# One-hots of a pair of edge chunks 8 to 56 nodes wide by its place in the list, and 88 counted rows for 90

## The chip, the cores and the metric

The kernel runs on one core of a Trainium2 chip. The metric is the device time of one execution in microseconds. PE is the matrix engine (its weight loads are listed apart, as PEld), DVE the vector engine, ACT the scalar engine, POOL the GpSimd engine and SP the engine that here only issues DMAs.

## What is computed

A graph layer on 12,500 nodes with 64 features and 400,000 edges, sorted by their target node `dst`. Targets are drawn as 12500·u², so low nodes have many edges and high nodes few.

```python
msg = node_feat[src] + edge_feat
agg = segment_sum(msg, dst, num_segments=12500)
h = relu(agg @ W1 + b1)
y = h @ W2 + b2
out = layernorm(x + y)
```

## The kernel before

The edge list is cut into 625 **chunks** of 640 edges, five chunks to a **row**, 125 rows. Since the list is sorted, the targets of one chunk lie in a short run of nodes from the chunk's first one.

Edge features are always summed by chunk. For a chunk, DVE writes a **one-hot** (edge by node of the run, `mark`, L887), PE multiplies the chunk's edge features with it (`products`, L1134) into PSUM, and DVE adds the result onto the run's columns of the transposed sums `lists` (`add`, L912). The one-hot's width is `w`: the run of nodes it can hold. Two chunks make a pair, with one `mark` and one interleaved series of products; two pairs make a **quad**, after whose marks DVE may fetch the first nodes of a new row into registers (`load_offsets`, L901, a register load whenever a chunk number is a multiple of 5). The adds of a quad are issued ahead of the marks of the next quad.

The node features `x[src]` of a chunk come in one of two ways. The last chunks of the list (175 before) are **gathered**: POOL issues five indirect DMAs for each (L613), and PE multiplies two operands, `gmsg` and `xmsg`, with the one-hot. The first `CROWS` rows are **counted**: no row of `x` is fetched. Instead, DVE compares each target's slice of the list with node numbers (`make_slot`, two compares L943 and L947 a slot, up to 12 passes of one node or 6 of two), PE turns these into counts of sources per target (`count_piece`, L1152), ACT copies the counts out of PSUM (L737), and PE multiplies them, in blocks of up to 128 targets, with `x` split in three bf16 parts (`multiply`, L1169, 98 matmuls a block). There are 647 slots in 43 groups of up to 128 passes, and 52 blocks.

One order is planned for all engines (`timeline`). It walks the slots; at some slots (`JOBS_AT`) a quad stands ahead of the slot, and the gathers (`GATHERS_AT`) are spread over the slots by a planned pace `PACE` per gathered chunk. Every engine runs its own part of that order, tied by semaphores: `RING` = 3 slots deep for one-hots of slots, 5 gathered and 6 counted chunks deep for edge data. For each group POOL also issues one indirect DMA for the `records` (L622), three slots behind the DVE search (L839, L844) that gives its offsets.

In the kernel before, a pair is `SLIM` = 32 wide if it is counted and in the first 76 rows, otherwise 64. All gathered pairs are 64 wide. A pair that proves wider than its one-hot is found at the start (`over`, L870) and sends the whole sum through a slow loop at the end. After the last slot come the last block's 98 matmuls, the signs that decide on this loop, and then the two dense layers and the norm (L1237 on), which the change does not touch.

Lines of the trace: 887 one-hots, 901 register loads, 912 adds, 943 and 947 compares of a slot, 1134 products by chunk, 1152 counting, 1169 blocks, 613 gathers, 622 records.

Of the kernel before, what the change touches and what calls it, by code (L numbers as in the profile page):

```python
# [8 lines left out]
P = 128  # L9
LN_EPS = 1e-5  # L10
PARTS = 3
TOP = 256
CROWS = 90
SLOT = 12
FINE = 16
RARE = 1e-7
PACE = 7.4

Unit = namedtuple("Unit", "first width nodes block row passes")
Slot = namedtuple("Slot", "group col n width key_cols pieces")  # L20
# [81 lines left out]
def narrow_chunks(n_nodes, n_edges, chunk, wide, most):  # L102

    before = lambda n: n_edges * math.sqrt(min(n, n_nodes) / n_nodes)
    count = 0
    while count < most:
        at = chunk * (count + 1)
        node = math.ceil(n_nodes * ((at + 5.5 * math.sqrt(at * (1 - at / n_edges))) / n_edges) ** 2)
        mean = before(node + wide) - before(node + 1)
        tail = mean - chunk  # L110
        if tail <= 0 or math.exp(-tail * tail / (2 * mean)) > RARE:
            break
        count += 1
    return count
# [42 lines left out]
def build(nc, x, src, dst, edge_attr, w1, b1, w2, b2, out):  # L157
    f32, i32, i16, bf16 = mybir.dt.float32, mybir.dt.int32, mybir.dt.int16, mybir.dt.bfloat16
    f16 = mybir.dt.float16
    ALU, ACT, AX = mybir.AluOpType, mybir.ActivationFunctionType, mybir.AxisListType  # L160

    N, D = x.shape
    E = src.shape[0]
    HID = w1.shape[1]
    TILES = 5
    CHUNK = P * TILES
    NCH = E // CHUNK
    ROWS = NCH // TILES
    ROW = TILES * CHUNK
    RT = TILES * TILES  # L170
    CCH = CROWS * TILES
    GCH = NCH - CCH
# [3 lines left out]
    SHIFT = 6  # L176
    WIN = 1 << SHIFT
    NWIN = -(-N // WIN)
    SLIM = WIN // 2
    NARROW_ROWS = narrow_chunks(N, E, CHUNK, SLIM, CCH) // TILES  # L180
    width_of = lambda kind, i: SLIM if kind == "count" and (i | 1) < NARROW_ROWS * TILES else WIN

    HI = -(-N // P)
    LOG_P = P.bit_length() - 1
# [8 lines left out]
    FINES = ROW // FINE  # L193
    CFINE = CROWS * FINES
    UNITS, SLOTS, WINDOWS, RANGES = plan(N, E, COUNTED, HI)
# [8 lines left out]
    DENSE = [u for u, x in enumerate(UNITS) if max(x.passes) * P > TOP]  # L204
# [70 lines left out]
    with ExitStack() as ctx:  # L275
        def sb(name, shape, dt=f32):
            return ctx.enter_context(nc.sbuf_tensor(name, shape, dt))
# [13 lines left out]
        counts = [sb(f"counts{k}", [P, HI * P], bf16) for k in range(2)]  # L291
        x_parts = sb("x_parts", [P, HI * XC], bf16)
        degrees = sb("degrees", [P, BLOCKS])
        over = sb("over", [P, len(DENSE) + TILES])
        rel_t = sb("rel_t", [P, NCH * TILES], i16)
        idx_t = sb("idx_t", [P, GCH * TILES], i32)
        idx_redo = sb("idx_redo", [P, TILES], i32)
# [21 lines left out]
        span_i = sb("span_i", [ROWS, TILES], i32)  # L319
# [18 lines left out]
        stage = x_parts[0:ROWS, 0:HI * PARTS * D].bitcast(f32)  # L338
        src_f, hi = stage[:, 0:ROW], stage[0:CROWS, ROW:2 * ROW]
        record_out = counts[0][0:CROWS, 0:FINES * REC].bitcast(f32).rearrange("t (b k) -> t b k", k=REC // 2)  # L340
        pad_out = onehot[0][:, 0:5 * REC // 2]
# [38 lines left out]
        src_copied, src_scaled, wide_seen = sem("src_copied"), sem("src_scaled"), sem("wide_seen")  # L380
# [86 lines left out]
        def _(sp):  # L467
# [22 lines left out]
            sp.wait_ge(most_made, 1)  # L490
            for a, b in in_sixteens(CROWS):
                sp.dma_start(most_dram[a * FINES:b * FINES].rearrange("(t k) -> t k", k=FINES), most[a:b, :]).then_inc(most_out, 16)
# [9 lines left out]
            sp.wait_ge(records_made, 2)  # L502
            for a, b in in_sixteens(CROWS):
                sp.dma_start(record_dram[a * FINES:b * FINES, :].rearrange("(t b) k -> t (b k)", b=FINES),
# [297 lines left out]
        def _(dve):  # L802
# [54 lines left out]
            for g in range(EARLY_GROUPS):  # L857
# [9 lines left out]
            nc.vector.tensor_scalar(chunk_out[:, 0, :], span_i[:, :], SHIFT, None, ALU.arith_shift_right).then_inc(chunk_made, 1)  # L867
            nc.vector.tensor_copy(chunk_out[:, 1, :], least[:, :]).then_inc(chunk_made, 1)
            dve.wait_ge(over_zeroed, 1)
            nc.vector.tensor_scalar(over[0:NARROW_ROWS, len(DENSE):], span_i[0:NARROW_ROWS, :], float(SLIM), None,  # L870
                                    ALU.is_ge).then_inc(wide_seen, 1)
            subtract(0)
            dve.wait_ge(turned["rel"], NTURNS["rel"])
            nc.vector.memset(lists[:, 2 * ROW:3 * ROW], 0.0).then_inc(agg_zeroed, 1)
# [83 lines left out]
            for s in range(NS + 1):  # L958
# [20 lines left out]
                if s in (3, 7):  # L979
                    k = s // 4  # L980
# [4 lines left out]

            dve.wait_ge(unit_kept, len(EVICTED))
            dve.wait_ge(unit_checked, len(DENSE))
            dve.wait_ge(wide_seen, 1)
            dve.wait_ge(degrees_kept, BLOCKS)
            dve.wait_ge(signs_made, 2)  # L990
            nc.vector.tensor_reduce(signs[:, 0:1], degrees[:, :], axis=AX.X, op=ALU.add).then_inc(signs_made, 1)
# [293 lines left out]
```

## Time and profile before

| | us |
|---|---|
| median of 3 runs | 1513.98 (1513.83 to 1514.28) |
| the profiled execution | 1512.37 |
| its span in the trace | 1510.5 |
| start, to the first one-hots | 0 to about 64 |
| slots 0 to 332 | about 64 to 815 |
| slots 333 to 618 | 815 to 1347 |
| slots 619 to 646, last block, signs | 1347 to 1418 |
| dense layers and norm | 1418 to 1510 |

The boundaries are the starts of the L947 instruction of slots 333 and 619 on DVE, and of the first L1237 on PE. The profiled execution has 1.9 us outside its span. The time of each engine in these five stretches is the first thing to read; the second is what DVE does between two slots, where a quad stands.

### The profile page before, as it was taken

Reading aid. Unit: us, or ns where it says so; the run is one execution under the profiler, and the core shown is the slowest. Engines: PE = TensorE matmul, PEld = TensorE weight load, DVE = VectorE, ACT = ScalarE, POOL = GpSimd, SP = SyncE. Lnnn points to the kernel's source line nnn. Section 1 sums busy time; section 2 is a strip of 40 time slices with the busy share of each in tenths; the row PEclk is TensorE's granted clock in tenths of the full one; section 3 lists DMA queues with packets and bytes.
Section 4 is the critical chain, followed back from the end, with each engine's and each line's share of the span. In section 5 each row is a group of like instructions: output and inputs, shape, how many; then the busy total and the mean of one; then the engine's idle time right before and its main releaser. Section 6 shows DMA issues by size and latency. Waiting matters only on the chain.

```text
span 1510.5 us, 47689 instructions
## 1 busy us (share of the span) xinstructions
PE 1249.6 (83%) x18983; PEld 1127.1 (75%) x18984; DVE 1297.0 (86%) x2753; ACT 781.5 (52%) x983; POOL 917.9 (61%) x995
## 2 busy tenths in 40 slices
PE   1366777887898989898989999999999999999873
PEld 1255666776787978797878888888888888988652
DVE  5499999999999989999999888988988899999243
ACT  3833322333454544555455666666666666666352
POOL 6746666766766666666756666665565666574132
PEclk8567899999998989999999999999999999999975
DMA  6734444444443434444444343434443443432132
GB/s 167 166 86 109 119 105 123 117 111 113 108 122 96 123 100 106 118 105 113 110 112 105 101 114 96 111 95 108 105 109 97 106 109 100 114 98 64 22 84 65
DMA packets 156582, 159.78 MB, mean 106 GB/s; under 512 B 52041, under 2 KB 141337, under 8 KB 156025
## 3 DMA queue, kind: packets, MB, share of 16 engines
q1 hardware_dynamic: 126301, 123.81, 28.2%
q0 software_dynamic: 30064, 32.96, 12.0%
q8 instruction: 151, 2.47, 0.7%
q14 instruction: 66, 0.54, 0.1%
HBM read 151.69 MB, written 4.97 MB: 104 GB/s over the span
## 4 chain that ended last, share of the span: by engine, by line
PE 46%; DVE 27%; issue 15%; DVEq 5%; POOL 2%; ACT 2%; DMA 1%; POOLq 0%; SPq 0%
PE sums_ps L1169 22%; PE counted_ps L1152 13%; DVE oh_key L947 11%; PE chunk_ps L1134 9%; DVE oh_lo L943 7%; DVEq L901 3%; DVE onehot L887 2%; DVE lists L912 2%; ACT counts L737 2%; POOL xmsg L613 1%; DVE less_b L839 1%; DVEq L912 1%; POOL x_parts L654 1%; DVE counts L956 1%; DVEq L905 1%
## 5 line engine op out<-in xcount | busy, mean ns | idle before, releaser
L613 POOL DMA_INDIRECT xmsg<-in_x,idx_t x875 | 837.7, 957 | 284.1 <-issue 260.0
L737 ACT CAST counts<-counted_ps 128x784 bf16<-128x784 f32 (+3 forms) x767 | 647.3, 860 | 524.5 <-PE counted_ps L1152 521.1
L1152 PE MATMUL counted_ps<-oh_key,oh_lo 128*128 128x98 bf16 (+1 forms) x5397 | 596.4, 231 | 153.3 <-DVE oh_key L947 117.1
L1169 PE MATMUL sums_ps<-x_parts,counts 128*128 128x193 bf16 (+3 forms) x5096 | 655.4, 254 | 0.5 <-issue 0.2
L1152 PEld LDWEIGHTS counted_ps<-oh_key,oh_lo 128*128 128x128 bf16 x5397 | 387.2, 101 | 218.2 <-DVE oh_key L947 159.5
L943 DVE TENSOR_TENSOR oh_lo<-chunk_ps,tables 128x768 bf16<-128x768 f16 (+2 forms) x647 | 456.5, 706 | 55.3 <-PE counted_ps L1152 33.2
L1169 PEld LDWEIGHTS sums_ps<-x_parts,counts 128*128 128x128 bf16 (+3 forms) x5096 | 473.9, 118 | 6.8 <-issue 4.4
L947 DVE TENSOR_TENSOR oh_key<-chunk_ps,tables 128x1176 bf16<-128x1176 f16 (+1 forms) x647 | 477.4, 738 | 0.0
L887 DVE TENSOR_TENSOR onehot<-chunk_ps,rel_t 128x320 f32<-128x320 f32 (+1 forms) x313 | 179.8, 616 | 5.1 <-issue 0.4
L1134 PE MATMUL chunk_ps<-onehot,cmsg 128*64 128x32 f32 (+1 forms) x4500 | 170.9, 230 | 14.8 <-DVE lists L912 8.4
L1134 PEld LDWEIGHTS chunk_ps<-onehot,cmsg 128*64 128x64 f32 x4500 | 156.3, 146 | 32.1 <-issue 15.7
L622 POOL DMA_INDIRECT records<-edge_records,run_at x43 | 40.6, 944 | 213.8 <-DVE run_at L844 213.2
L912 DVE TENSOR_TENSOR lists<-lists,chunk_ps 64x32 f32 (+1 forms) x625 | 122.4, 196 | 26.0 <-PE chunk_ps L1134 5.8
L1134 PE MATMUL chunk_ps<-onehot,gmsg 128*64 128x64 f32 x1750 | 76.5, 239 | 7.0 <-issue 3.6
L712 ACT ACTIVATE tables<-turn_ps,zero 128x512 f16<-128x512 f32 x43 | 29.5, 687 | 94.4 <-PE turn_ps L1106 94.4
L1134 PEld LDWEIGHTS chunk_ps<-onehot,gmsg 128*64 128x64 f32 x1750 | 65.4, 150 | 14.6 <-issue 8.2
L1134 PE MATMUL chunk_ps<-onehot,xmsg 128*64 128x64 f32 x1750 | 72.0, 232 | 0.0
L660 POOL TENSOR_TENSOR x_parts<-x_parts,b_all 128x512 f32<-128x512 f32 (+1 forms) x13 | 15.6, 1201 | 81.7 <-DMA x_parts<-in_x 81.7
L1134 PEld LDWEIGHTS chunk_ps<-onehot,xmsg 128*64 128x64 f32 x1750 | 64.8, 149 | 0.0
L1247 PEld LDWEIGHTS chunk_ps<-w_sb,x_parts 128*128 128x128 f32 x196 | 30.5, 241 | 24.0 <-issue 13.6
L1038 DVE TENSOR_TENSOR x_parts<-chunk_ps,x_parts 128x512 f32<-128x512 f32 (+1 forms) x13 | 8.6, 661 | 42.8 <-POOL x_parts L654 32.2
L1247 PE MATMUL chunk_ps<-w_sb,x_parts 128*128 128x64 f32 x196 | 31.1, 326 | 15.2 <-ACT x_parts L774 15.2
(104 smaller groups left out, 462.8 us busy)
## 6 DMA issues: line engine op xcount, KB each, us to landing
cmsg<-in_edge_attr SPq DMA_DIRECT2D x450, 160.0 KB
gmsg<-in_edge_attr SPq DMA_DIRECT2D x175, 160.0 KB
xmsg<-in_x,idx_t POOLq DMA_INDIRECT x875
x_parts<-in_x SPq DMA_DIRECT2D x12, 256.0 KB, 3.3
out_nodes<-x_parts SPq DMA_DIRECT2D x12, 256.0 KB, 2.6
edge_records<-counts SPq DMA_DIRECT2D x1, 1500.0 KB
lists<-in_src SPq DMA_DIRECT2D x1, 1400.0 KB
lists<-in_dst SPq DMA_DIRECT2D x1, 1400.0 KB
```

The lines of the kernel that those rows point to most:

```text
L613: pool.indirect_dma_start(xmsg[:, at * D:(at + 1) * D], None, x, bass.IndirectOffsetOnAxis(ap=idx_t[:, of:of + 1], axis=0)).then_inc(gathe ...
L622: pool.indirect_dma_start(records[g % 2][:, :], None, record_dram, bass.IndirectOffsetOnAxis(ap=run_at[g % 2][:, 0:1], axis=0)).then_inc(r ...
L737: nc.scalar.copy(to.rearrange("p h (m n) -> p h m n", m=m), ps.rearrange("p m (n h) -> p h m n", h=HI)).then_inc(unit_kept, 1)
L887: nc.vector.tensor_tensor(onehot[place // 2 % OSLOTS][:, 0:n * w].rearrange("p (j n) -> p j n", j=n), node_ps[:, 0:w].unsqueeze(1).broadca ...
L901: dve.load(at_regs[kind][i // TILES % 2], chunk_out[row:row + 1, 1, :])
L912: nc.vector.tensor_tensor(to, to, pair_ps[place // 2 % 2][place % 2 * D:(place % 2 + 1) * D, 0:w], ALU.add).then_inc(added, 1)
L943: nc.vector.tensor_tensor(oh_lo[s % RING][:, 0:n * P].rearrange("p (k n o) -> p k n o", k=n, o=2), lo_ps.rearrange("p (n o) -> p n o", o=2 ...
L947: nc.vector.tensor_tensor(oh_key[s % RING][:, 0:n * w].rearrange("p (k n o) -> p k n o", k=n, o=2), key_ps[:, 0:w].rearrange("p (n o) -> p ...
L1134: mm = nc.tensor.matmul(pair_ps[place // 2 % 2][half * D:(half + 1) * D, 0:w], of[:, j * D:(j + 1) * D], onehot[place // 2 % OSLOTS][:, (h ...
L1152: mm = nc.tensor.matmul(unit_ps[u][:, col:col + slot.key_cols], oh_lo[s % RING][:, n * P:(n + 1) * P], oh_key[s % RING][:, n * slot.key_co ...
L1169: mm = nc.tensor.matmul(sums_ps[0:n, 0:XC], counts[b % 2][:, h * P:h * P + n], x_parts[:, h * XC:(h + 1) * XC], start=(h == 0), stop=(h == ...
L1247: mm = nc.tensor.matmul(chunk_ps[k][:, i * D:(i + 1) * D], hid[k][:, i * P:(i + 1) * P], w2_sb[:, :], start=(i == 0), stop=(i == n - 1), s ...
```

## The change

The width of a pair's one-hot now follows from its chunk number in the whole list: `narrow_chunks` is asked for each width 8, 16, ... 56 how many chunks from the list's start are safely narrower, and a pair takes the smallest width that holds. The gathered pairs, which stand at the list's end, take part. `CROWS` falls from 90 to 88, so 440 chunks are counted and 185 gathered; `PACE` falls from 7.4 to 7.0 us a gathered chunk. The check of spans at the start is made once for each width.

```diff
-CROWS = 90
+CROWS = 88
-PACE = 7.4
+PACE = 7.0
...
-    SLIM = WIN // 2
-    NARROW_ROWS = narrow_chunks(N, E, CHUNK, SLIM, CCH) // TILES
-    width_of = lambda kind, i: SLIM if kind == "count" and (i | 1) < NARROW_ROWS * TILES else WIN
+    NARROW_ROWS = {w: narrow_chunks(N, E, CHUNK, w, NCH) // TILES for w in range(8, WIN, 8)}
+    NARROW_ROWS = {w: rows for w, rows in NARROW_ROWS.items() if rows}
+
+    def width_of(kind, i):
+        c = (i | 1) + (CCH if kind == "gather" else 0)
+        return next((w for w, rows in NARROW_ROWS.items() if c < rows * TILES), WIN)
...
-        over = sb("over", [P, len(DENSE) + TILES])
+        over = sb("over", [P, len(DENSE) + len(NARROW_ROWS) * TILES])
...
-            nc.vector.tensor_scalar(over[0:NARROW_ROWS, len(DENSE):], span_i[0:NARROW_ROWS, :], float(SLIM), None,
-                                    ALU.is_ge).then_inc(wide_seen, 1)
+            for k, (w, rows) in enumerate(NARROW_ROWS.items()):
+                at = len(DENSE) + k * TILES
+                nc.vector.tensor_scalar(over[0:rows, at:at + TILES], span_i[0:rows, :], float(w), None,
+                                        ALU.is_ge).then_inc(wide_seen, 1)
...
-            dve.wait_ge(wide_seen, 1)
+            dve.wait_ge(wide_seen, len(NARROW_ROWS))
```

What `plan`, `narrow_chunks` and `timeline` give with these numbers:

| | before | after |
|---|---|---|
| counted pairs, by width | 190 of 32, 35 of 64 | 40 of 8, 50 of 16, 50 of 24, 50 of 32, 30 of 40 |
| gathered pairs, by width | 87 of 64 | 20 of 40, 52 of 48, 18 of 56, 2 of 64 |
| single gathered chunk | 64 | 64 |
| counting passes, slots, groups, blocks | 5397, 647, 43, 52 | 5264, 622, 42, 50 |
| quads ahead of slots 0 to 332 (with 0, 1, 2 register loads) | 25, 56, 8 | 27, 56, 9 |
| quads ahead of slots 333 to 618 | 17, 39, 5 | 17, 41, 5 |
| quads after that, without the single chunk | 2, 4, 0 | 1, 0, 0 |
| gathers at slots 0 to 332, 333 to 618, after | 507, 336, 32 | 554, 367, 4 |

Slots 0 to 618 are the same in both kernels, word for word; the 25 slots that are gone stood at the end.

On DVE, at the first slots (chunk sums of the first quads; each `L912 ISA` is a register operation of the add below it), before:

```order
L912 TENSOR_TENSOR lists<-lists,chunk_ps 64x64
L912 ISA
L912 TENSOR_TENSOR lists<-lists,chunk_ps 64x32
L912 ISA
L912 TENSOR_TENSOR lists<-lists,chunk_ps 64x32
L887 TENSOR_TENSOR onehot<-chunk_ps,rel_t 128x320
L887 TENSOR_TENSOR onehot<-chunk_ps,rel_t 128x640
L943 TENSOR_TENSOR oh_lo<-chunk_ps,tables 128x1536
L947 TENSOR_TENSOR oh_key<-chunk_ps,tables 128x1176
```

and in the changed kernel, at the same place:

```order
L918 TENSOR_TENSOR lists<-lists,chunk_ps 64x40
L918 ISA
L918 TENSOR_TENSOR lists<-lists,chunk_ps 64x8
L918 ISA
L918 TENSOR_TENSOR lists<-lists,chunk_ps 64x8
L893 TENSOR_TENSOR onehot<-chunk_ps,rel_t 128x80
L893 TENSOR_TENSOR onehot<-chunk_ps,rel_t 128x400
L949 TENSOR_TENSOR oh_lo<-chunk_ps,tables 128x1536
L953 TENSOR_TENSOR oh_key<-chunk_ps,tables 128x1176
```

The number of instructions of a quad stays; the marks shrink from 320 and 640 columns to 80 and 400, the adds from 32 and 64 to 8 and 40.

The same engine further on, where a quad carries a register load, in the changed kernel:

```order
L893 TENSOR_TENSOR onehot<-chunk_ps,rel_t 128x400
L893 TENSOR_TENSOR onehot<-chunk_ps,rel_t 128x640
L907 TENSOR_LOAD chunk_out
L949 TENSOR_TENSOR oh_lo<-chunk_ps,tables 128x768
L953 TENSOR_TENSOR oh_key<-chunk_ps,tables 128x1176
```

The load stands between the marks and the next slot's compares, as before.

On PE, the end of the counting, in the changed kernel (slots 617 to 621, the last quad, the single chunk, the last block):

```order
L1158 MATMUL counted_ps<-oh_key,oh_lo 128x196 x8
L1175 MATMUL sums_ps<-x_parts,counts 128x193 x49
L1158 MATMUL counted_ps<-oh_key,oh_lo 128x196 x2
L1175 MATMUL sums_ps<-x_parts,counts 128x193 x16
L1158 MATMUL counted_ps<-oh_key,oh_lo 128x196 x2
L1175 MATMUL sums_ps<-x_parts,counts 128x193 x16
L1158 MATMUL counted_ps<-oh_key,oh_lo 128x196 x2
L1175 MATMUL sums_ps<-x_parts,counts 128x193 x17
L1158 MATMUL counted_ps<-oh_key,oh_lo 128x196 x6
L1140 MATMUL chunk_ps<-onehot,cmsg 64x40 x10
L1140 MATMUL chunk_ps<-onehot,gmsg 64x64 x10
L1140 MATMUL chunk_ps<-onehot,xmsg 64x64 x10
```

and before, at the end:

```order
L1169 MATMUL sums_ps<-x_parts,counts 128x193 x5
L1134 MATMUL chunk_ps<-onehot,cmsg 64x64 x10
L1134 MATMUL chunk_ps<-onehot,gmsg 64x64 x10
L1134 MATMUL chunk_ps<-onehot,xmsg 64x64 x10
L1152 MATMUL counted_ps<-oh_key,oh_lo 128x294 x5
L1134 MATMUL chunk_ps<-onehot,gmsg 64x64 x5
L1134 MATMUL chunk_ps<-onehot,xmsg 64x64 x5
L1180 MATMUL turn_ps<-ident,sums 64x128
L1169 MATMUL sums_ps<-x_parts,counts 87x193 x98
```

The passes over three nodes are gone, and the block before the last is multiplied in two slots, 49 and 49 matmuls, and not spread over ten.

## Rows read from the trace of the kernel before

**Rows 1.** The five stretches: busy us (instructions) of each engine, PE clock, DMA share, GB/s

```profile
0.00:64.50 64.50, 16.52 (x110) 12.78 (x112) 29.06 (x36) 35.82 (x22) 44.94 (x79) 0.69 0.75 179
64.50:815.50 751.00, 614.58 (x10344) 561.71 (x10341) 702.81 (x1421) 334.34 (x408) 489.45 (x515) 0.90 0.42 110
815.50:1347.40 531.90, 496.26 (x7396) 454.25 (x7394) 478.84 (x1108) 341.01 (x457) 331.70 (x352) 0.99 0.39 103
1347.40:1418.40 71.00, 63.09 (x900) 57.63 (x896) 50.34 (x127) 34.04 (x49) 23.85 (x27) 0.99 0.25 64
```

**Rows 2.** Who waited for whom, 64.5 to 815.5 us: total, times, longest

```profile
POOL records L622 <- DVE run_at L844: 112.9, 27, 16.8
PE counted_ps L1152 <- DVE oh_key L947: 104.0, 121, 7.5
DVE oh_lo L943 <- PE counted_ps L1152: 12.3, 18, 1.7
```

**Rows 3.** The same view, 815.5 to 1347.4 us

```profile
DVE oh_lo L943 <- PE counted_ps L1152: 19.6, 38, 1.8
PE counted_ps L1152 <- ACT counts L737: 15.0, 36, 0.7
PE counted_ps L1152 <- DVE oh_key L947: 12.3, 20, 1.2
```

**Rows 4.** Groups by line and shape, whole span: busy us, mean ns of one

```profile
L887 DVE TENSOR_TENSOR onehot<-chunk_ps,rel_t 128x640 f32<-128x640 f32 x122 | 98.0, 820 | 1.8
L887 DVE TENSOR_TENSOR onehot<-chunk_ps,rel_t 128x320 f32<-128x320 f32 x191 | 88.0, 486 | 3.3 <-issue 0.4
L870 DVE TENSOR_SCALAR over<-span_i 76x5 f32<-76x5 int32 x1 | 0.2, 168 | 0.0
```

**Rows 5.** Register loads of L901: duration min/median/max ns

```profile
L901 DVEq TENSOR_LOAD <-chunk_out x125: 1180/1240/1494, 60.6 to 1388.9; - x125
```

**Rows 6.** DVE in order of time: start us, us; a quad without a load

```profile
238.60 0.89 DVE L912 TENSOR_TENSOR lists<-lists,chunk_ps 64x32 f32 x4
239.51 0.89 DVE L887 TENSOR_TENSOR onehot<-chunk_ps,rel_t 128x320 f32<-128x320 f32 x2
240.32 0.95 DVE L943 TENSOR_TENSOR oh_lo<-chunk_ps,tables 128x1536 bf16<-128x1536 f16 x1
...
1236.53 1.56 DVE L887 TENSOR_TENSOR onehot<-chunk_ps,rel_t 128x640 f32<-128x640 f32 x2
1238.00 0.27 DVE L934 TENSOR_TENSOR lists<-lists,turn_ps 64x128 f32<-64x128 f32 x1
```

**Rows 7.** DVE in order of time: quads with one load, then one with two

```profile
140.88 0.89 DVE L887 TENSOR_TENSOR onehot<-chunk_ps,rel_t 128x320 f32<-128x320 f32 x2
142.05 0.96 DVE L943 TENSOR_TENSOR oh_lo<-chunk_ps,tables 128x1536 bf16<-128x1536 f16 x1 [0.28 <-issue]
...
304.66 0.89 DVE L912 TENSOR_TENSOR lists<-lists,chunk_ps 64x64 f32 x4
305.58 1.23 DVE L887 TENSOR_TENSOR onehot<-chunk_ps,rel_t 128x320 f32<-128x320 f32 x2
307.00 0.56 DVE L943 TENSOR_TENSOR oh_lo<-chunk_ps,tables 128x768 bf16<-128x768 f16 x1 [0.20 <-issue]
...
172.00 1.22 DVE L887 TENSOR_TENSOR onehot<-chunk_ps,rel_t 128x320 f32<-128x320 f32 x2
174.63 0.86 DVE L839 TENSOR_SCALAR_CACHE_REDUCE less_b<-most_b,node_t 128x620 bf16<-128x620 int16 x1 [1.41 <-issue]
```

**Rows 8.** PE in order of time, at full clock

```profile
1004.29 0.80 PE L1134 MATMUL chunk_ps<-onehot,gmsg 128*64 128x64 f32 x20
1004.92 0.75 PE L1134 MATMUL chunk_ps<-onehot,xmsg 128*64 128x64 f32 x20
1005.51 0.72 PE L1134 MATMUL chunk_ps<-onehot,cmsg 128*64 128x32 f32 x20
1006.17 0.33 PE L1105 MATMUL turn_ps<-ident,keys 128*128 128x128 f32 x1
...
1014.60 0.33 PE L1152 MATMUL counted_ps<-oh_key,oh_lo 128*128 128x196 bf16 x2
1014.77 0.50 PE L1169 MATMUL sums_ps<-x_parts,counts 128*128 128x193 bf16 x4
1015.10 0.33 PE L1152 MATMUL counted_ps<-oh_key,oh_lo 128*128 128x196 bf16 x2
```

**Rows 9.** The end in order of time, PE, ACT and DVE

```profile
1397.37 0.29 DVE L947 TENSOR_TENSOR oh_key<-chunk_ps,tables 128x294 bf16<-128x294 f16 x1
1401.42 0.21 DVE L912 TENSOR_TENSOR lists<-lists,chunk_ps 64x64 f32 x1 [3.77 <-PE chunk_ps L1134]
1402.85 0.80 PE L1134 MATMUL chunk_ps<-onehot,gmsg 128*64 128x64 f32 x10
1405.66 8.59 PE L1169 MATMUL sums_ps<-x_parts,counts 128*87 128x193 bf16 x98
1414.28 0.15 ACT L751 COPY degrees<-sums_ps 87x1 f32<-87x1 f32 x1 [10.90 <-PE sums_ps L1169]
```

**Rows 10.** POOL: the gathers' durations min/median/max ns, and two beside a long DVE instruction

```profile
L613 POOL DMA_INDIRECT xmsg<-in_x,idx_t x875: 939/944/4197, 22.0 to 1387.6; - x175
...
68.22 6.75 DVE L956 TENSOR_TENSOR counts<-counts,x_parts 128x3136 f32<-128x3136 f32 x2
...
69.33 3.11 POOL L613 DMA_INDIRECT xmsg<-in_x,idx_t  x1 [0.30 <-issue]
72.75 3.03 POOL L613 DMA_INDIRECT xmsg<-in_x,idx_t  x1 [0.30 <-issue]
76.09 0.94 POOL L613 DMA_INDIRECT xmsg<-in_x,idx_t  x1 [0.30 <-issue]
```

**Rows 11.** The wait of DVE at the start, 0 to 64.5 us

```profile
DVE lows L852 <- DMA records<-edge_records,run_at: 17.3, 1, 17.3
```

## The prediction

> **What bounds the kernel now.** I read the five stretches first [rows 1]. From 64.5 to 815.5 us (slots 0 to 332) DVE is busy 703 of 751 us and PE 615; PE is short of one-hots, since it waits 104 us for L947, while DVE waits only 12 us for PE [rows 2]. The 48 us in which DVE is not busy are no slack: most of them stand behind quads, as rows 7 shows below. So DVE alone sets this stretch. From 815.5 to 1347.4 us (slots 333 to 618) PE is busy 496 of 532 us at a granted clock of 0.99 of the upper level, 2.4 GHz, and DVE 479; each waits a little for the other, DVE 19.6 us for PE and PE 12.3 us for DVE [rows 1, 3]. This stretch is bound by both. The last slots and the closing blocks take 71 us [rows 1]. What matters therefore is what the change takes from DVE before 815 us, from both engines until 1347 us, and from the chain of work after that.
>
> The second thing to read is a quad on DVE. Four adds, two marks, and the next slot follows. Where no register load stands behind the marks, the next instruction starts 0.81 us after the first of two 32-wide marks (239.51 to 240.32), and 1.47 us after the first of two 64-wide ones (1236.53 to 1238.00) [rows 6]: 0.15 us and 1.03 ns for each of 640 or 1280 columns. Where a load stands behind them, it does not follow the width. Two 32-wide marks then take 1.17 us (140.88 to 142.05), a 64- and a 32-wide one 1.42 us (305.58 to 307.00), each with idle time ahead of the next slot, and with two loads it is 2.63 us (172.00 to 174.63) [rows 7]. The load itself takes 1.18 us at the least, 1.24 at the median and 1.49 at most [rows 5]; it leaves while the marks begin, and DVE gets no new work until it is back. I took this distance for all quads from the timeline. With one load the means are 1.27 us for 46 quads of 32 and 32, 1.34 for 37 of 32 and 64, 1.47 for 16 of 64 and 64; with two loads 2.69 for 12 of the mixed ones. Only 44 of the 156 whole quads, and the single chunk, carry no load. This is where the change's promise goes: narrower marks run inside the load's time.
>
> **Marks, slots 0 to 332.** Before, the 89 quads take 120.8 us from their first mark to the next instruction. After, 27 quads without a load cost 0.15 us plus 1.03 ns a column each, by their widths 19.4 us (the 25 of before 26.1); 56 with one load cost the load's time, for which I take 1.27 us, the value of the narrowest marks that the trace has, 70.6 us; 9 with two cost 2.6 us each, 23.4. Together 113.4 us, 7.4 less. By the busy time alone it would look far more: 27.8 thousand columns fewer at the slope between 486 ns for 320 columns and 820 ns for 640 [rows 4], or 29 us. An 8-wide mark (80 columns) is in no row. Its bounds are 0.15 us, the part that doesn't depend on columns, and 0.49 us, the 320-column row; I take 0.24 us, since both 320 and 640 columns lie on one line. The upper end for all narrow marks would return 7 us.
>
> **Adds.** A quad of four 32-wide adds takes 0.89 us up to its first mark (51 quads), one of 64-wide adds 0.99 (16 quads); rows 6 and 7 show 0.91 and 0.92 with the one above and below. That is 0.78 us and 1.6 ns for each column of its two pair widths. The sum of pair widths falls from 7296 to 4512 in the first stretch, 4.5 us less, and three quads more cost 2.3 us. First stretch in all: -7.4 - 4.5 + 2.3 = **-9.6 us**.
>
> **Slots 333 to 618.** DVE: marks 81.5 for 84.8 us by the same working, adds 1.4 us less and two quads more 1.6 us, -3.1 in all. PE: its products don't become shorter. 20 records of 64-wide `gmsg` take 0.63 us from start to start, 20 of 32-wide `cmsg` 0.66 us (1005.51 to 1006.17) [rows 8]: a narrower one-hot gives PE nothing. But 8 more gathered chunks stand here (74 for 66), at 20 records or 0.63 us each, +5.0 us. Where both engines bound, the truth lies between -3.1 and +5.0; I take **+1 us**, the middle. The same extra chunks in the first stretch (8 gathered, 4 counted, 6.3 us of PE) are covered by PE's waits for L947 [rows 2]. Without that cover they would cost these 6.3 us.
>
> **The end.** Before, 71.0 us pass from slot 619 to the first L1237. After, three slots, one quad and the single chunk remain. PE has then to do: 16 counting matmuls and 49 + 98 of blocks. At full clock 2 counting matmuls take 0.17 us and 4 of a block 0.33 [rows 8], and the last 98 took 8.6 us, or 88 ns each [rows 9]: 1.4 + 12.9 us. The quad's 60 records take 1.9 us [rows 8], the single chunk 1.5 (1402.85 us on) and three turned sums 1.2. From the last block's end to L1237 are 4.1 us [rows 9]. PE enters behind DVE by the 49 matmuls of slot 618, 4.3 us, and I allow 3 us for waits such as the 3.8 us of the last adds [rows 9]. The sum is 30.3 us, so the stretch gives 40.7 us; I take **-40**, with 36 and 43 as ends by the allowance for waits.
>
> **Start and POOL.** Six more compares of 0.17 us each [rows 4] stand ahead of DVE's wait of 17.3 us for the first records [rows 11]; that wait hides all 1.0 us, and without it they would cost it. POOL issues 50 gathers more. One issue takes 0.94 us and 0.30 us to the next, 1.25 in all. The first stretch gets 47 more (554 for 507), 59 us, and loses 10 us of length: 69 us, against 112.9 us in which POOL waits for DVE's search [rows 2]. 16.8 us of these are one wait at the start, so 27 us remain. In slots 0 to 96 the cover is thinnest: 14 gathers or 17.5 us against 21 us of waits after the first. I cost POOL at nothing; in the trace of before nothing on DVE waits for it later.
>
> The edit on `over` and the longer reduction at the end are columns of a few elements and cost nothing.
>
> **Sum.** -9.6 + 1 - 40 = -48.6 us. The profiled execution took 1512.4 us (a span of 1510.5); less 48.6 it is 1463.8, and the median of the runs shown is 1.6 us above it, so the forecast is **1465 us**, 3.2% faster. Four fifths of that are the 25 slots that are no longer there, not the narrow one-hots.
>
> **Rival A: the load hides in the narrow marks.** If the idle time behind the marks stays as it is and the marks' own time comes off in full, the two long stretches lose 37.6 us on DVE in place of 10.7, 27 us more: 1438 us. For it speaks that with one load 37 mixed quads take 1.34 us against 1.27 for narrower ones, so some of the width shows. Against it: that 0.33 us of marks bought only 0.07. Chance 0.10. The Trainium skill ("DMA: Bandwidth & Descriptors", Latency and other measured facts) gives a `tensor_load` floor of about 600 ns. With that, loads would end under marks of 0.6 us or more and this rival would hold; no load in the trace was under 1180 ns, so I follow the rows.
>
> **Rival B: part of it is given back.** POOL's cover runs out in slots 0 to 96 and PE waits for `xmsg`, or PE's 11 us of added chunk work show. For it: the thin cover above, and groups with a wait under 3 us. Against: five chunks of buffer. Price 6.3 + 5.0 - 1 for PE and up to 10 us for POOL, so 1475 to 1486. Chance 0.16.
>
> **Rival C, slower than before: POOL becomes the bound.** From about 96 us to the end of slot 332 POOL has some 542 issues in 706 us, so it decides from 1.30 us an issue on, against 1.25 now. Slower than before it needs 51 us more, that is 1.40 us; at 1.45 both long stretches go by POOL and the time is about 1560. For it: two gathers beside the 6.75 us of DVE L956 took 3.11 and 3.03 us [rows 10]. Against it: the median of 875 stands 5 ns above the minimum, so compares, marks and adds of DVE don't disturb it. Chance 0.03. [...]
>
> **Rival D: the change doesn't do what it says.** If a chunk were wider than its one-hot, the slow loop over 625 chunks would run, at a PE-DVE round trip of over a microsecond each, and the time would pass 2000 us. For the inputs the widest spans are 6, 12, 19, 26, 32, 39 and 43 nodes where 8 to 56 are allowed. Chance under 0.01.
>
> **How the numbers follow.** Forecast 0.67, A 0.10, B 0.16, C 0.03, the rest (about no change, or a slower clock of PE) 0.04. The forecast's own ends are 1454 (36 to 43 at the end, DVE's -3.1, marks as taken) and 1476 (the upper end of narrow marks, +5.0). The range reaches to half of A's way and most of B: 1446 to 1482. A measurement of this kernel tells 0.2% from no change; faster by more 0.94, within 0.02, slower 0.04.
>
> **What would show it.** Right: slot 333's L947 starts some 9 us before 815; slots 333 to 618 take 529 to 537 us; slot 619 to L1237 takes 28 to 35 us; L901 stays at a median of 1.2 to 1.4 us, with more idle time by "issue" ahead of L943 though marks are shorter; busy DVE falls by 80 us or more while the span falls by about 49; records of L1134 stay at 31 ns from start to start. Wrong: idle time of DVE ahead of L943 that doesn't grow (A), waits of PE for `xmsg` or of DVE for `records` (B, C), a granted clock well under 0.90 in the first long stretch.

## The result and the profile of the changed kernel

The changed kernel takes **1468.3 us** (median of 4 runs, 1467.2 to 1471.3) against 1514.1 us before (4 runs, 1513.8 to 1514.3). The ratio is 0.970, with a 95% interval of 0.968 to 0.972. The forecast was 1465 us with a range of 1446 to 1482. The profiled execution took 1467.2 us with a span of 1465.4, so the span fell by 45.1 us.

The stretches of the changed kernel, cut at the same instructions (L947 is now L953, L1237 is L1243). The columns are those of [rows 1]: length, then busy us and instructions of PE, PEld, DVE, ACT and POOL, granted clock of PE, DMA share, GB/s:

```profile
64.40:815.00 750.60, 627.46 (x10538) 574.11 (x10537) 672.14 (x1439) 334.08 (x408) 535.97 (x560) 0.88 0.43 114
815.00:1345.20 530.20, 497.78 (x7558) 458.76 (x7556) 471.54 (x1121) 340.82 (x457) 358.70 (x380) 0.99 0.40 108
1345.20:1373.90 28.70, 22.84 (x301) 21.61 (x300) 8.98 (x34) 4.72 (x8) 0.00 (x0) 1.00 0.09 19
1373.90:1465.40 91.50, 58.03 (x246) 39.91 (x246) 35.89 (x65) 36.31 (x49) 28.02 (x26) 0.72 0.28 65
```

| | before | after | forecast of the difference | measured |
|---|---|---|---|---|
| slots 0 to 332 | 751.1 | 750.6 | -9.6 | -0.5 |
| slots 333 to 618 | 531.9 | 530.2 | +1 | -1.7 |
| slot 619 to the dense layers | 71.0 | 28.7 | -40 | -42.3 |
| dense layers, norm | 92.1 | 91.5 | 0 | -0.6 |

(The lengths of before are taken between the starts of the instructions, so that of slots 0 to 332 differs by 0.1 from [rows 1].) The first stretch is the one that surprised: DVE's busy time there fell from 702.8 to 672.1 us [rows 1], 31 us, and the stretch became half a microsecond shorter.

Where those 31 us went is in the groups of DVE in slots 0 to 332. The columns are busy us, mean ns of one, and behind the bar the idle time ahead of such instructions with what ended it. Two groups of the kernel before, then the changed kernel:

```profile
L943 DVE TENSOR_TENSOR oh_lo<-chunk_ps,tables 128x1536 bf16<-128x1536 f16 (+3 forms) x334 | 289.5, 867 | 29.5 <-issue 17.2 <-PE counted_ps L1152 12.3
L887 DVE TENSOR_TENSOR onehot<-chunk_ps,rel_t 128x320 f32<-128x320 f32 (+1 forms) x176 | 94.6, 579 | 2.9 <-issue 0.2
```

```profile
L949 DVE TENSOR_TENSOR oh_lo<-chunk_ps,tables 128x1536 bf16<-128x1536 f16 (+3 forms) x334 | 289.4, 867 | 50.9 <-issue 30.0 <-PE counted_ps L1158 20.7
L953 DVE TENSOR_TENSOR oh_key<-chunk_ps,tables 128x1176 bf16<-128x1176 f16 (+2 forms) x333 | 245.6, 737 | 0.0
L893 DVE TENSOR_TENSOR onehot<-chunk_ps,rel_t 128x160 f32<-128x160 f32 (+4 forms) x182 | 66.8, 409 | 2.8
L918 DVE TENSOR_TENSOR lists<-lists,chunk_ps 64x16 f32 (+4 forms) x364 | 63.9, 176 | 15.2 <-DVE lists L918 2.7
```

DVE stands idle for 50.9 us ahead of L949, the first compare of a slot, 21.4 us more than before; ahead of the adds by chunk it is 4.0 us more (15.2 for 11.2) and ahead of the adds of finished blocks, L940, 5.0 us more (5.5 for 0.5). Counted behind the marks, whatever instruction follows, the idle time was 25.6 us before and is 51.4 now (taken from the timeline for each quad, as all such distances below). The register loads have kept their length:

```profile
L907 DVEq TENSOR_LOAD <-chunk_out x125: 1181/1241/1481, 60.6 to 1341.1; - x125
```

A quad with one load and a quad with none, DVE in order of time (start, duration, instruction, idle time before it in brackets):

```profile
145.17 0.84 DVE L918 TENSOR_TENSOR lists<-lists,chunk_ps 64x8 f32 x4
146.05 0.39 DVE L893 TENSOR_TENSOR onehot<-chunk_ps,rel_t 128x80 f32<-128x80 f32 x2
147.44 0.69 DVE L949 TENSOR_TENSOR oh_lo<-chunk_ps,tables 128x1024 bf16<-128x1024 f16 x1 [1.00 <-PE counted_ps L1158]
...
151.90 0.80 DVE L918 TENSOR_TENSOR lists<-lists,chunk_ps 64x8 f32 x4
152.73 0.72 DVE L893 TENSOR_TENSOR onehot<-chunk_ps,rel_t 128x400 f32<-128x400 f32 x2
153.37 0.95 DVE L949 TENSOR_TENSOR oh_lo<-chunk_ps,tables 128x1536 bf16<-128x1536 f16 x1
```

The two 8-wide marks take 0.39 us, and the next instruction starts 1.39 us after the first. An 8-wide and a 40-wide mark, 480 columns, take 0.64 us where no load stands behind them. So the quad with far less work is the longer one. The idle 1.00 us is put down to PE's counting here. The quad's own load tells otherwise (duration, then start):

```profile
L907 DVEq TENSOR_LOAD <-chunk_out x1: 1414/1414/1414, 145.9 to 145.9; - x1
```

It starts 0.14 us before the first mark and ends at 147.32 us, and L949 starts 0.12 us later. The kernels with the loads moved, below, confirm it.

The waits of slots 0 to 332 (total us, times, longest):

```profile
PE counted_ps L1158 <- DVE oh_key L953: 99.9, 123, 7.0
...
POOL records L626 <- DVE run_at L848: 50.9, 23, 9.0
DVE oh_lo L949 <- issue: 30.0, 31, 2.4
DVE oh_lo L949 <- PE counted_ps L1158: 20.7, 26, 3.4
...
DVE lists L940 <- issue: 5.5, 8, 1.2
```

PE waits for DVE nearly as long as before (104.0 us in [rows 2]). POOL's wait for the search has shrunk from 112.9 to 50.9 us and has not run out. In slots 333 to 618 DVE's wait for PE grew from 19.6 us [rows 3] to

```profile
DVE oh_lo L949 <- PE counted_ps L1158: 37.1, 66, 1.7
```

### The profile page after: what moved, and what is told of

It is laid out like the page before. It is cut to its first block, busy times and chain, and to the rows that moved or that the text cites. A ratio compares the mean times of both kernels' runs of the same rounds, so it can differ in the third digit from the quotient of the medians.

```text
span 1465.4 us, 47112 instructions
## 1 busy us (share of the span) xinstructions
PE 1223.0 (83%) x18748; PEld 1107.5 (76%) x18749; DVE 1217.6 (83%) x2696; ACT 751.7 (51%) x941; POOL 967.6 (66%) x1043
## 4 chain that ended last, share of the span: by engine, by line
PE 44%; DVE 28%; issue 17%; DVEq 5%; ACT 3%; DMA 2%; POOL 1%; POOLq 0%; SPq 0%
PE sums_ps L1175 20%; PE counted_ps L1158 12%; DVE oh_key L953 11%; PE chunk_ps L1140 10%; DVE oh_lo L949 8%; DVEq L907 3%; ACT counts L741 3%; DVE lists L918 2%; DVE onehot L893 2%; DMA lists<-in_dst 1%; DVEq L918 1%; POOL x_parts L658 1%; DVE less_b L843 1%; DMA edge_records<-counts 1%; PE turn_ps L1186 1%
## 5 line engine op out<-in xcount | busy, mean ns | idle before, releaser
L617 POOL DMA_INDIRECT xmsg<-in_x,idx_t x925 | 888.4, 960 | 292.4 <-issue 275.0
L741 ACT CAST counts<-counted_ps 128x784 bf16<-128x784 f32 (+2 forms) x728 | 618.3, 865 | 500.8 <-PE counted_ps L1158 494.3
L1175 PE MATMUL sums_ps<-x_parts,counts 128*128 128x193 bf16 (+3 forms) x4900 | 629.0, 254 | 0.3
L949 DVE TENSOR_TENSOR oh_lo<-chunk_ps,tables 128x768 bf16<-128x768 f16 (+3 forms) x622 | 444.6, 715 | 94.6 <-PE counted_ps L1158 57.8
L953 DVE TENSOR_TENSOR oh_key<-chunk_ps,tables 128x1176 bf16<-128x1176 f16 (+2 forms) x622 | 459.5, 739 | 0.0
L1140 PE MATMUL chunk_ps<-onehot,cmsg 128*64 128x16 f32 (+4 forms) x4400 | 167.3, 222 | 6.3 <-DVE lists L918 5.3
L918 DVE TENSOR_TENSOR lists<-lists,chunk_ps 64x48 f32 (+6 forms) x625 | 113.8, 182 | 30.5 <-PE chunk_ps L1140 8.4
L893 DVE TENSOR_TENSOR onehot<-chunk_ps,rel_t 128x480 f32<-128x480 f32 (+6 forms) x313 | 134.7, 472 | 4.8
L1140 PE MATMUL chunk_ps<-onehot,gmsg 128*64 128x48 f32 (+3 forms) x1850 | 79.6, 237 | 6.3 <-issue 3.5
L1140 PE MATMUL chunk_ps<-onehot,xmsg 128*64 128x48 f32 (+3 forms) x1850 | 77.2, 234 | 0.0
```

Source lines behind the costliest of these rows:

```text
L617: pool.indirect_dma_start(xmsg[:, at * D:(at + 1) * D], None, x, bass.IndirectOffsetOnAxis(ap=idx_t[:, of:of + 1], axis=0)).then_inc(gathe ...
L741: nc.scalar.copy(to.rearrange("p h (m n) -> p h m n", m=m), ps.rearrange("p m (n h) -> p h m n", h=HI)).then_inc(unit_kept, 1)
L893: nc.vector.tensor_tensor(onehot[place // 2 % OSLOTS][:, 0:n * w].rearrange("p (j n) -> p j n", j=n), node_ps[:, 0:w].unsqueeze(1).broadca ...
L918: nc.vector.tensor_tensor(to, to, pair_ps[place // 2 % 2][place % 2 * D:(place % 2 + 1) * D, 0:w], ALU.add).then_inc(added, 1)
L949: nc.vector.tensor_tensor(oh_lo[s % RING][:, 0:n * P].rearrange("p (k n o) -> p k n o", k=n, o=2), lo_ps.rearrange("p (n o) -> p n o", o=2 ...
L953: nc.vector.tensor_tensor(oh_key[s % RING][:, 0:n * w].rearrange("p (k n o) -> p k n o", k=n, o=2), key_ps[:, 0:w].rearrange("p (n o) -> p ...
```

## The experiments

Three theories were on the table. **Theory 1:** a register load keeps DVE from the next slot for some 1.3 us whatever the marks' width, so the narrow one-hots give little, and the gain is the 25 slots that are gone. **Theory 2:** the narrow one-hots carry the gain. **Theory 3:** PE or POOL sets the first long stretch, and what DVE saves would be lost with or without the loads.

### Parts alone, and the loads moved

Two kernels with one part of the change each:

```diff
# w1_widths_only, against the changed kernel
-CROWS = 88
+CROWS = 90
-PACE = 7.0
+PACE = 7.4
# w2_rows_only, against the kernel before
-CROWS = 90
+CROWS = 88
-PACE = 7.4
+PACE = 7.0
```

And two in which the loads stand behind the next slot's two compares, in the changed kernel (m1_loads_later, runs b and c the same file) and in the kernel before (m2_before_loads_later):

```diff
                     for k in range(0, len(quad), 2):
                         mark(quad[k:k + 2])
-                    load_offsets(quad)
+                    if s == NS:
+                        load_offsets(quad)
...
                 if s < NS:
                     make_slot(s)
+                    load_offsets(JOBS_AT[s])
```

> The change's widths (8 to 56 by chunk number) with the 90 counted rows and the pace of 7.4 of the kernel before: the same 647 slots. Theory 1 (the register load of about 1.3 us sets the time of 7 quads in 10, so narrow marks buy little; the gain is the slots that are gone): 1504 to 1510 us, that is 4 to 10 us under the kernel before, with more idle time behind the marks (about 60 us in place of 35). Theory 2 (the narrow one-hots carry the gain): 1475 us or less.

> 88 counted rows and a pace of 7.0, with the widths of the kernel before (32 or 64): 622 slots. Theory 1: nearly the whole gain, 1472 to 1480 us, somewhat over the changed kernel because the 64-wide gathered quads that moved forward cost DVE their width where no load stands behind them. Theory 2: 1500 us or more.

> The changed kernel with the register loads of a quad issued behind the two compares of the next slot, not ahead of them, so that 1.15 to 1.7 us of DVE work stand in the queue while the load runs. The number of loads, marks and slots is the same. Theory 1: the 67 us of idle time behind the marks of slots 0 to 618 nearly vanish; the stretch of slots 0 to 332 loses 35 to 45 us, the next one 5 to 12, where PE bounds too: 1418 to 1430 us. Theory 3 (PE or POOL, not DVE, sets the first stretch of the changed kernel, so that what the load costs is covered): 1460 to 1468 us, with DVE waiting for PE instead.

> The kernel before with the same move of the loads. Theory 1: 35 us of idle time behind its marks are to be had, some 25 to 30 of them in time: 1482 to 1492 us. The distance to m1_loads_later is then larger than the 46 us between the two kernels, since the narrow marks now count: 55 to 70 us. Theory 3: 1508 to 1514 us.

> The same kernel as m1_loads_later again (the changed kernel with its register loads behind the next slot's compares), for a pair with a kernel before that takes its usual 1514 us. Theory 1 (the loads, not the marks, set the quads): 1418 to 1430 us. Theory 3 (PE or POOL sets the first stretch of the changed kernel): 1460 to 1468 us.

> The changed kernel with the register loads of a quad behind the two compares of the next slot, once more beside a kernel before. If the kernel before takes its 1514 us, theory 1 (the loads set the quads): 1418 to 1430 us; theory 3 (PE or POOL sets the first stretch of the changed kernel): 1460 to 1468 us. If the kernel before takes about 2400 us again, PE and ACT, not DVE, are what is waited for and every theory expects a ratio within 1.5% of 1.

On the three chips that ran these six, the kernel before itself took 2373, 2401 and 2403 us, not 1514. The ratios to it were 1.001 (w1, 0.999 to 1.003), 1.006 (w2, 1.004 to 1.008), 1.004 (m1, 1.002 to 1.005), 0.997 (m2, 0.995 to 0.998), 1.009 (m1 b, 1.006 to 1.012) and 1.009 (m1 c, 1.006 to 1.012). The waits of m1_loads_later, whole span, tell why no theory can be judged by these times:

```profile
ACT counts L741 <- remote: 651.1, 103, 19.2
...
DVE oh_lo L949 <- PE counted_ps L1160: 358.4, 167, 11.3
...
PEld counted_ps L1160 <- issue: 323.2, 258, 10.3
```

PE pauses by "issue", that is, without a wait that the profile shows, for 1.3 us on average and up to 10.3 (the last row, of its weight loads), and DVE and ACT wait for PE. A stretch of PE's order of time shows two such pauses:

```profile
408.68 0.41 PE L1177 MATMUL sums_ps<-x_parts,counts 128*125 128x193 bf16 x3
412.33 0.34 PE L1160 MATMUL counted_ps<-oh_key,oh_lo 128*128 128x196 bf16 x2 [3.23 <-issue]
412.51 0.42 PE L1177 MATMUL sums_ps<-x_parts,counts 128*125 128x193 bf16 x3
414.85 0.83 PE L1160 MATMUL counted_ps<-oh_key,oh_lo 128*128 128x196 bf16 x4 [1.92 <-issue]
```

What makes PE pause was not found. These six totals are inconclusive on the three theories. Only distances inside DVE, where nothing of PE's stands between, can be used. The median distance from a quad's first mark to the next instruction, in us, by its loads and the sum of its four chunks' widths:

| | no load, 96 | one, 64 | one, 96 | one, 128 | one, 192 | two, 192 |
|---|---|---|---|---|---|---|
| before | - | - | - | 1.20 | 1.39 | 2.67 |
| m2_before_loads_later | - | - | - | 0.82 | 1.14 | 1.14 |
| changed kernel | 0.64 | 1.24 | 1.40 | 1.24 | 1.20 | - |
| m1_loads_later | 0.64 | 0.47 | 0.64 | 0.81 | 1.14 | - |

With the load moved, a quad with a load takes what the same widths take without one, and the distance follows the width; with the load in its old place it does not. (The quads of four 8-wide chunks are left out: on these chips DVE waits behind them and their median is 1.41 us; with the same move on a chip with the usual time it is 0.30.) So the distance is the load's. What it is worth in the whole kernel was still open.

### PE and POOL made light

The next four ran on a chip where the kernel before took 1514.2 us. In all four PE and POOL do only part of their work, so that DVE alone can set the time: a chunk's products are cut to the first and the last matmul, the counting to one matmul a piece, a block to 2 of its 98 matmuls, and one of a chunk's five gathers is issued; the slow loop is switched off. DVE and ACT do all they did. The core of the edit, the same in all four:

```diff
-                        if n < len(steps[half]):
+                        if n < len(steps[half]) and n in (0, len(steps[half]) - 1):
...
                 for h in range(h0, h1):
+                    if h not in (0, HI - 1):
+                        continue
...
                 for k, j in GATHERS_AT[s]:
-                    gather(k, j)
+                    if j == TILES - 1:
+                        gather(k, j)
```

l0_before is the kernel before with this, l1_widths has the new widths with 90 rows, l2_after is the changed kernel, and l3_after_later is l2_after with the loads moved as above.

> The kernel before with PE and POOL lightened, so that only DVE is left as a bound: of the products of a chunk only the first and the last matmul, one counting matmul a piece in place of one a pass, 2 of 98 matmuls a block, one gather of five; the slow loop is switched off at the end. What DVE does is unchanged. This is the base for the three others: from the sums of slots, marks, loads and adds 1297 us of DVE path, and some 180 us of start, x parts and closing layers, 1460 to 1485 us.

> The same lightening with the change's widths alone (90 counted rows, pace 7.4, the same 647 slots). Theory 1 (a quad with register loads takes the loads' 1.3 us each, whatever its marks): 15 to 25 us under l0_before, from 44 quads without a load, the 16 widest with one, and the adds. Theory 2 (narrow marks and adds count in full on the path of DVE): 45 to 55 us under it.

> The same lightening of the changed kernel (widths, 88 rows, pace 7.0). Both theories: 25 slots, one group and two blocks less than l1_widths, 27 + 3 us. Theory 1: 45 to 55 us under l0_before, more than half of it the slots; theory 2: 75 to 85 us under it.

> l2_after with the register loads of a quad behind the two compares of the next slot. Theory 1: the loads' cover is back and the narrow marks count: 65 to 80 us under l2_after. Theory 2 (the loads cost nothing in l2_after): within 10 us of it.

| | median us | ratio to the kernel before | slots 0 to 332 | marks to next instruction there |
|---|---|---|---|---|
| l0_before | 1460.0 | 0.964 (0.963 to 0.966) | 744.0 | 121.0 |
| l1_widths | 1437.6 | 0.950 (0.948 to 0.951) | 733.6 | 114.3 |
| l2_after | 1399.8 | 0.925 (0.923 to 0.926) | 741.7 | 119.1 |
| l3_after_later | 1334.6 | 0.881 (0.880 to 0.883) | 692.3 | 59.8 |

With PE's busy time in the first stretch down from 627 to 494 us and POOL's from 536 to 126, that stretch still takes 741.7 us in l2_after against 750.6 in the changed kernel:

```profile
63.15:804.89 741.74, 493.69 (x2481) 172.96 (x2481) 670.21 (x1439) 332.96 (x408) 125.83 (x134) 0.59 0.34 96
```

That answers Theory 3 for the most part: PE and POOL together are worth 9 us there. The widths give 22.4 us (l0 to l1), where Theory 1 wanted 15 to 25 and Theory 2 45 to 55. The loads give 65.2 (l2 to l3), Theory 1's 65 to 80 at its lower edge. One number missed both theories: l2_after is 60.2 us under l0_before, where Theory 1 wanted 45 to 55 and Theory 2 75 to 85. The widths' part of it was as Theory 1 had it; the slots, group and blocks that are gone gave 37.8 us (l1 to l2) where 30 had been worked out for both.

The step from l1 to l2 also shows a loss that the sum had too small: in slots 0 to 332 the new rows and pace **add** 8.1 us, 4.8 of it in the marks' column and 3.0 in the adds, since three more quads, two of them without a load and one with two, are planned into the same slots. So of 10.4 us that the widths save there, 2.3 remain.

### The two that count, on chips with the usual times

The kernel before took 1514.4 us on this chip.

> The changed kernel with the register loads of a quad behind the two compares of the next slot; nothing is left out. The lightened kernels showed 65 us for this move where DVE alone bounds. If DVE alone bounded slots 0 to 332 of the changed kernel too, 1418 to 1430 us. If PE and POOL, which have 8 gathered chunks more there, take over soon after (theory 3), less than half of it comes: 1440 to 1465 us, with DVE waiting for PE ahead of L949 by 60 us or more in all.

> The change's widths with the 90 counted rows and the pace of 7.4 of the kernel before, nothing left out. The lightened pair gave 22 us for the widths. In the full kernel PE has its part from slot 333 on, so fewer come: 1498 to 1508 us. If the widths carried the change's gain it would be 1475 us or less.

**w1_widths_only_b** took 1503.9 us, 0.994 of before (0.993 to 0.996). The widths alone are worth 10.5 us: 5.2 in slots 0 to 332 (745.9 us), 4.9 in slots 333 to 618 (527.0). The other 35 of the change's 46 us come with the rows, by difference; the rows alone were not timed on such a chip.

**m1_loads_later_d** took 1426.2 us, 0.941 of before (0.940 to 0.943). That is 42 us less than the changed kernel, and the fastest that computes everything. The profiled execution is the fastest of its five, 1420.6 us (the others took 1421.9 to 1426.9), so its stretches flatter the move by some 5 us:

```profile
61.70:775.30 713.60, 622.35 (x10583) 574.96 (x10580) 667.99 (x1439) 335.02 (x408) 534.91 (x561) 0.89 0.46 120
775.30:1298.60 523.30, 497.68 (x7557) 458.34 (x7556) 469.54 (x1120) 340.65 (x457) 359.93 (x382) 0.99 0.41 110
1298.60:1327.00 28.40, 22.89 (x301) 21.66 (x300) 9.03 (x34) 4.57 (x8) 0.00 (x0) 1.00 0.09 20
```

37.0 us come from the first stretch and 6.9 from the second, of 46.7 between the two spans. The same groups of DVE in the first stretch, and the same quad as at 145.17 us above:

```profile
L949 DVE TENSOR_TENSOR oh_lo<-chunk_ps,tables 128x1536 bf16<-128x1536 f16 (+3 forms) x334 | 289.1, 866 | 11.7 <-PE counted_ps L1160 8.4 <-issue 3.0
L893 DVE TENSOR_TENSOR onehot<-chunk_ps,rel_t 128x160 f32<-128x160 f32 (+4 forms) x182 | 66.8, 409 | 2.9
```

```profile
138.29 0.84 DVE L918 TENSOR_TENSOR lists<-lists,chunk_ps 64x8 f32 x4
139.16 0.39 DVE L893 TENSOR_TENSOR onehot<-chunk_ps,rel_t 128x80 f32<-128x80 f32 x2
139.47 0.68 DVE L949 TENSOR_TENSOR oh_lo<-chunk_ps,tables 128x1024 bf16<-128x1024 f16 x1
```

Marks and compares have the same busy time to 0.3 us. What changed is the idle time ahead of L949, 11.7 us for 50.9, and the distance of this quad, 0.31 us for 1.39. The loads themselves are as long as ever (median 1.24 us); behind two compares, which in most slots keep DVE busy for 1.2 or 1.6 us, they cost little. After 26 of the 125 DVE still stands idle until the load is back, 11.3 us in all, 6.5 of them in this stretch. The 1.00 us that the trace of the changed kernel put down to PE has gone too, with PE's work unchanged: it was the load's.

The new limit of this kernel is in its waits, slots 0 to 332:

```profile
DVE oh_lo L949 <- PE counted_ps L1160: 8.4, 11, 2.6
DVE lows L856 <- DMA records<-edge_records,run_at: 8.3, 4, 3.6
```

DVE now waits for records, which it did only at the start before. POOL's own wait for the search is down to 8.1 us from 50.9: its cover, on which the forecast rested, is used up by this edit, not by the change.

## Why the forecast was right, and where it wasn't

**The end: right.** -42.3 us against -40. PE at the close of the changed kernel:

```profile
1345.16 4.36 PE L1175 MATMUL sums_ps<-x_parts,counts 128*128 128x193 bf16 x49
...
1354.66 0.78 PE L1140 MATMUL chunk_ps<-onehot,cmsg 128*64 128x40 f32 x20
...
1360.97 0.43 PE L1186 MATMUL turn_ps<-ident,sums 128*64 128x128 f32 x2 [1.44 <-DVE sums L932]
1361.29 8.55 PE L1175 MATMUL sums_ps<-x_parts,counts 128*56 128x193 bf16 x98
```

The matmuls of the blocks and the time from the last block to L1243 (1369.8 to 1374.0, 4.1 us) came as worked out. The waits ahead of the last block were 2.3 us, 0.87 for the adds and 1.44 for the sums, where 3 were allowed. The whole stretch was 28.7 us for a sum of 30.3.

**Slots 0 to 332: the mechanism right, its size not.** "Narrower marks run inside the load's time" is what the trace shows, and the stretch is DVE's. The sum of -9.6 us came out as -0.5. The step that failed is the price of what remains once marks are narrow: two counts, and a rest.

- Marks with loads: 56 quads with one load took 1.33 us each, not 1.27, and the 9 with two 2.82, not 2.6. Quads without a load came as forecast (19.1 us for 19.4). Together 118.9 us for 113.4: 5.5 of the miss, 3.9 from the quads with one load and 2.0 from those with two, less 0.3 from the others. Two small slips are in it: 56 times 1.27 is 71.1, not 70.6, and 2.6 lies under the mean of 2.69 that the forecast itself had read for two loads. The main cause stands in the trace of before too: the loads come in two lengths, 1.18 to 1.26 us and 1.40 to 1.49 us. Behind the narrow marks of the changed kernel the distance is the load's length: 1.20 us on average in the 59 quads with one short load, 1.43 in the 38 with one long load. The 1.27 us came from 46 quads of which 15 had a long load; in this stretch of the changed kernel 31 of 56 have one (28 of 56 before). What makes a load long stays open.
- Adds: 0.90 us a quad on average, 0.93 before. Taken with the three more quads, the time from the first add to the first mark is 81.8 us for 81.7, +0.2 instead of -2.2: 2.4 of the miss. The slope of 1.6 ns a column was about right (the median quad fell from 0.92 to 0.88 us), but more of the quads have a wait among their adds. A quad of 8-wide adds still takes 0.84 us: four adds in a row start 0.21 us apart though one lasts only 0.158:

```profile
L918 DVE TENSOR_TENSOR lists<-lists,chunk_ps 64x8 f32 x80 | 12.7, 158 | 4.1 <-DVE lists L918 1.3
```

- The rest. The two above make 7.9 of the 9.1 us. In the light kernels the same step (l0 to l2) gives 2.3 us for the forecast's 9.6, so 7.3 of the miss is there without PE's and POOL's full work, and 1.8 appears only with it. It doesn't stand ahead of L949: there the changed kernel idles 5.3 us more than its light twin, and the kernel before 5.9 more than its own. Two profiles on two chips don't tell 1.8 us further apart.

The forecast had put all of PE's added work under its waits at no cost, and had nothing for PE's clock. That cover does fail somewhat in w1_widths_only_b, which saved 5.2 us in this stretch where its light twin saved 10.4. It has no added work there, 10340 matmuls for 10344 [rows 1], but a lower granted clock, 0.86 for 0.90, and PE is busy 13 us longer:

```profile
64.40:810.30 745.90, 627.62 (x10340) 576.18 (x10339) 667.02 (x1421) 334.56 (x408) 489.54 (x515) 0.86 0.42 111
```

Ahead of L949 it idles 9.8 us more than its light twin, 3.9 more than the kernel before does. So there the loss goes with PE's clock and not with more matmuls.

**Slots 333 to 618: within the bounds.** -1.7 us between the ends of -3.1 and +5.0; +1 had been taken. By the w1 run the widths save 4.9 us there, so by difference the rows cost about 3 of the 5.0 us of added PE work.

**Narrow products: right.** PE gains nothing from narrow one-hots. 20 records of 8 columns take 0.58 us from start to start, as 20 of 40 do:

```profile
122.64 0.75 PE L1140 MATMUL chunk_ps<-onehot,cmsg 128*64 128x8 f32 x20 [0.54 <-DVE lists L918]
123.22 0.79 PE L1140 MATMUL chunk_ps<-onehot,gmsg 128*64 128x40 f32 x20
123.80 0.79 PE L1140 MATMUL chunk_ps<-onehot,xmsg 128*64 128x40 f32 x20
```

The 8-wide mark, bounded by 0.15 and 0.49 us and taken at 0.24, is 237 ns. Of the signs that the forecast named, busy DVE fell by 79.4 us over the span for 80 or more, and the span by 45.1 for about 49. Slot 333 started at 815.0 us and not some 9 us before 815: this sign failed, with the first stretch.

**The rivals.** A (the load hides in the marks) fell: idle time behind marks doubled from 25.6 to 51.4 us. The Trainium skill ("DMA: Bandwidth & Descriptors", Latency and other measured facts) puts the floor of a `tensor_load` at about 600 ns. The forecast set against it that no load in the trace was under 1180 ns. That holds for the 125 loads of five numbers only; DVE's one load of a single number, at the end, took 537 ns before and 536 in the changed kernel, near that floor:

```profile
L1009 DVEq TENSOR_LOAD <-redo_i x1: 536/536/536, 1372.8 to 1372.8; - x1
```

What a load costs here had to be read from the rows of loads of its own kind. B (part given back through PE or POOL) is at most the 1.8 us above in the first stretch, and not through POOL. C: the 925 gathers kept their pace (median 944 ns), POOL still waited 50.9 us. D: the time is far under that of the slow loop.

**The balance.** The sum said -48.6 us, the spans -45.1: 9.1 us too much in the first stretch, 2.7, 2.3 and 0.6 too little in the others. That the total missed by 3.5 us and not by 9 is therefore luck. "Four fifths are the 25 slots" held roughly, by difference: about 35 of 46 us.

## What to carry to other kernels

Before shortening short vector work, look at what is issued behind it: measure from the start of an instruction to the start of the next one, once with and once without the register load, look at the load's own length, and cost the edit by that distance and not by busy time. A register load that must come back before the engine gets more work is best put behind the longest work already queued; here moving one call was worth 42 us, nearly as much as the whole change's 46. And when rows, groups or slots are taken from the end of a plan, recount what is planned into the stretch that stays: three quads that moved forward took back most of what the narrow one-hots had saved there (8.1 of 10.4 us in the light kernels).

## What the runs showed of the hardware that was not expected

The distance over a load has no order by width; it follows the load's own length. In the changed kernel a load starts 0.13 us before the quad's first mark (median of 97 quads with one load), and the next instruction of DVE starts 0.06 to 0.14 us after the load's end. The lengths fall in two groups, 70 loads of 1.18 to 1.26 us and 55 of 1.40 to 1.48 us; before, 74 and 51. Why there are two wasn't found. An idle time can be labelled with a far releaser though the engine's own load held it up: 1.00 us "<-PE" in the changed kernel vanished with the load moved.

PE's granted clock early in the run was lower in the changed kernel, while PE had about as much to do. Three windows from slots 0 to 96, before, then after:

```profile
100.00:150.00 50.00, 35.02 (x571) 30.88 (x572) 47.13 (x92) 22.07 (x39) 34.93 (x38) 0.74 0.44 115
150.00:200.00 50.00, 37.55 (x667) 33.24 (x665) 46.46 (x91) 17.61 (x28) 33.01 (x35) 0.86 0.43 112
200.00:250.00 50.00, 36.97 (x689) 32.47 (x685) 46.15 (x92) 13.71 (x16) 33.05 (x35) 0.93 0.44 115
```

```profile
100.00:150.00 50.00, 37.44 (x604) 32.88 (x601) 44.82 (x93) 21.41 (x39) 37.58 (x41) 0.70 0.45 121
150.00:200.00 50.00, 41.49 (x664) 37.38 (x665) 44.70 (x95) 18.53 (x29) 36.45 (x39) 0.74 0.46 126
200.00:250.00 50.00, 39.05 (x651) 35.08 (x650) 43.05 (x97) 13.70 (x16) 36.11 (x39) 0.84 0.40 111
```

Both levels of the clock (1.2 and 2.4 GHz) are in each window, the lower one more of the time after. From 150 to 250 us PE's busy time is 6 us longer with 41 matmuls fewer. The lower clock comes with the widths: w1_widths_only_b, which has them alone, shows a mean clock of 0.895 to 0.900 in its five runs, beside 0.910 to 0.916 in nine runs of the kernel before on the same chip (the changed kernel 0.898 to 0.906 in four). Why narrower one-hots should lower it wasn't found.

The largest surprise stays open. Three chips ran every kernel put on them at medians of 2365 to 2424 us, the kernel before included, with PE pausing by "issue", and none of these kernels' differences on DVE could be seen in their times there. The page of m1_loads_later lists 149 packets in the DMA queue for instructions, as many as that of the changed kernel at its usual time, so a larger number of them is not the reason.
